# Query and key projections of two blocks as seven block products in place of eight

## The reference

```python
qkv = x @ w_qkv.T                                   # 4096 x 512 by 512 x 1536
q, k, v = ...                                       # 16 heads of 32
q = q * cos + rotate_half(q) * sin                  # the same for k
scores = einsum(q, k) * scale                       # causal, window of 64
x = layernorm(x + softmax(scores) @ v @ w_out.T)
gate, up = silu((x @ w_gate) * s_gate), (x @ w_up) * s_up
x = layernorm(x + ((gate * up) @ w_down) * s_down)
```

## Time and profile before

| | before |
|---|---|
| median of 3 runs | 1202.55 us |
| profiled execution, its own time | 1202.61 us |
| its span (first to last instruction) | 1200.7 us |
| PE busy | 1186.8 us, 99% |
| DVE busy | 844.7 us, 70% |
| ACT busy | 572.7 us, 48% |
| POOL busy | 501.4 us, 42% |
| granted TensorE clock | 0.998 of full speed |

### The profile page before, as it was taken

One profiled execution on the slowest core, in us unless ns is written; L12 is line 12 of the kernel. 1 busy time (PEld: TensorE's weight loads), 2 busy tenths in 40 slices (PEclk: granted clock), 3 DMA queues, 4 the chain that ended last, 5 costly groups with the idle time before them and its releaser, 6 DMA issues.

```text
span 1200.7 us, 24567 instructions
## 1 busy us (share of the span) xinstructions
PE 1186.8 (99%) x8311; PEld 548.7 (46%) x8311; DVE 844.7 (70%) x2546; ACT 572.7 (48%) x1613; POOL 501.4 (42%) x488
## 2 busy tenths in 40 slices
PE   9899999999999999999999999999999999999997
PEld 4344444444444444444444444444444444444444
DVE  7888887548975499655996559865697657975534
ACT  3853883038820388104880149701596016850330
POOL 0745653145522555234561345514465134541330
PEclk9999999999999999999999999999999999999999
DMA  8999764086530855209651195412944139532000
GB/s 283 167 204 233 163 127 84 35 145 120 90 74 36 159 106 107 58 37 165 117 97 49 45 180 103 97 41 66 180 89 89 41 90 173 89 72 53 18 1 36
DMA packets 344409, 123.76 MB, mean 103 GB/s; under 512 B 309472, under 2 KB 328288, under 8 KB 344288
## 3 DMA queue, kind: packets, MB, share of 16 engines
q1 hardware_dynamic: 336128, 107.27, 46.0%
q10 hardware_dynamic: 5040, 8.59, 1.9%
q0 software_dynamic: 3120, 6.29, 1.8%
HBM read 26.69 MB, written 8.39 MB: 29 GB/s over the span
## 4 chain that ended last, share of the span: by engine, by line
PE 92%; DVE 2%; ACT 2%; DMA 1%; issue 1%; POOL 1%; SPq 0%; POOLq 0%; ACTq 0%
PE bank L625 45%; PE bank L770 18%; PE bank L631 16%; PE bank L649 8%; PE bank L732 3%; PE bank L712 2%; ACT bank L940 1%; DMA wqkv<-w_qkvT 1%; DMA xT_sb<-xT_sb 1%; DVE fuse L1052 0%; DVE fuse L1065 0%; POOL xT_sb L513 0%; POOL fuse L518 0%; ACT fuse L895 0%; ACT wu L895 0%
## 5 line engine op out<-in xcount | busy, mean ns | idle before, releaser
L625 PE MATMUL bank<-x1T,wg 128*128 128x512 f16 (+1 forms) x1032 | 242.5, 378 | 0.0
L625 PE MATMUL bank<-x1T,wu 128*128 128x512 f16 x1024 | 241.9, 379 | 0.0
L631 PE MATMUL bank<-wqkv,xT_sb 128*128 128x512 f32 x512 | 229.4, 596 | 0.0
L940 ACT ACTIVATE bank<-bank,neg_max,qk_scale 128x128 f32<-128x128 f32 x512 | 220.5, 435 | 13.0 <-DVE neg_max L1110 11.3
L770 PE MATMUL bank<-wd,fuse 128*128 128x512 f16 (+1 forms) x1056 | 222.4, 373 | 0.0
L518 POOL TENSOR_TENSOR fuse<-ffn_tmp,fuse 128x512 f16<-128x512 f32 x128 | 148.3, 1159 | 156.1 <-ACT fuse L895 155.2
L538 POOL TENSOR_TENSOR fuse<-fuse 128x512 f16<-128x512 f32 x116 | 132.1, 1167 | 129.6 <-ACT fuse L895 128.8
L895 ACT ACTIVATE fuse<-fuse 128x512 f16<-128x512 f32 x120 | 65.6, 618 | 248.2 <-DVE fuse L1060 247.1
L770 PEld LDWEIGHTS bank<-wd,fuse 128*128 128x128 f16 x1056 | 103.4, 98 | 120.3 <-issue 4.0
L513 POOL TENSOR_TENSOR xT_sb<-probs,xT_sb 128x512 f16<-128x512 f32 x112 | 129.7, 1158 | 65.7 <-ACT xT_sb L895 65.7
L625 PEld LDWEIGHTS bank<-x1T,wu 128*128 128x128 f16 x1024 | 100.2, 98 | 120.6
(11 more groups left out here) (147 smaller groups left out, 1097.2 us busy)
## 6 DMA issues: line engine op xcount, KB each, us to landing
xT_sb<-xT SPq DMA_DIRECT2D x32, 256.0 KB, 3.8
v_cross<-v_own SPq DMA_DIRECT2D x64, 128.0 KB, 2.6
out<-y ACTq DMA_DIRECT2D x32, 256.0 KB, 2.0
qkT<-x SPq DMA_DIRECT2D x28, 256.0 KB, 3.4
wqkv<-w_qkvT SPq DMA_DIRECT2D x2, 1024.0 KB, 8.4
wg<-w_gate POOLq DMA_DIRECT2D x1, 2048.0 KB, 9.1
wu<-w_up POOLq DMA_DIRECT2D x1, 2048.0 KB, 11.0
wd<-w_down POOLq DMA_DIRECT2D x1, 2048.0 KB, 9.0
```

The source lines that it names most:

```text
L625: last = pe.matmul(dst, lhsT, rhs, start=(i == 0), stop=(i == len(pairs) - 1))
L631: last = pe.matmul(dst, xT_sb[:, j, k, :], wqkv[:, k, cols], start=(k == 0), stop=(k == KC - 1))
L940: last = act.activation(unit, unit, ACT.Exp, bias=neg_max[:, s % 2, h // 3, h % 3:h % 3 + 1], scale=qk_scale[:, 2:3], accum_out=row_sum[:, ...
```

## The change

Two blocks of a tile make a pair (blocks 0 and 1, blocks 2 and 3). Their x is a 2 by 2 matrix of quarters (front or back block; low or high half of the 512 inputs), as is the q and k weight (low or high inputs; even or odd columns). Strassen's scheme in Winograd's form gives the four results from seven quarter products, with four sums of x, four of the weights and seven of the products.

- PE: `project_pair` replaces the even and odd products of two blocks. The order is products 1, 6, 5, 7, then 2 (after ACT has kept product 1, into the same bank), 3 (after DVE has read banks) and 4. In the body v 1 comes first, then pair 1, then v 2.
- POOL: four sums of x for each pair (`sum_x`, 128x256 each), ahead of `spread_maximum`; four sums of the weights, once (`sum_w`; in tile 0 at steps 9, 10 and 12, and one after `invert_deviation1(a, 2)`); two sums of kept products for each pair (`sum_back`), ahead of the pair's `split_low`.
- ACT: two copies from PSUM for each pair (`keep_products`): for pair 0 ahead of the last y store of the tile, for pair 1 after v 0 and v 1, ahead of the split of block 2.
- DVE: five sums for each pair, of a bank and a kept product. Two (`sum_second`) come before `carry_keys`, the tables and the last `finish_y`. Block 2i+1 reads its odd columns from `kept_products(i)[3]`, in SBUF (`fuse`, or `ffn_tmp`), where it read a bank.
- Tile 1's pair 0 is still made in `first` by the old functions, and tile 0 is unchanged. So 13 pairs change.
- In the diff `sum_x`, `sum_w` (128x1024 each step) and `sum_back` are POOL's, `project_pair` PE's, `keep_products` ACT's and `rope_pair` DVE's.
- The scratch for DMA descriptors made by POOL is set to 4 KB, which makes room for `w_sums`.

```diff
+        w_sums = sb("w_sums", [P, 3, KC // 2, EMB], F32)
+        def kept_products(i):
+            if i == 0:
+                return rope_other[0], rope_other[1], rope_other[3], rope_other[2]
+            return rope_t[0], ffn_tmp[:, 0, :], rope_t[1], ffn_tmp[:, 1, :]
...
+            def sum_x(a, i):
...
+                done(x_summed, pool.tensor_tensor(sums[:, 0, :, :], back_low, back_high, ALU.add))
+                done(x_summed, pool.tensor_tensor(sums[:, 2, :, :], front_low, back_low, ALU.subtract))
+                pool.wait_ge(x_summed[0], n + 1)
+                done(x_summed, pool.tensor_tensor(sums[:, 1, :, :], sums[:, 0, :, :], front_low, ALU.subtract))
+                pool.wait_ge(x_summed[0], n + 3)
+                done(x_summed, pool.tensor_tensor(sums[:, 3, :, :], front_high, sums[:, 1, :, :], ALU.subtract))
+            def sum_w(step):
...
+            def sum_back(a, i):
+                first, second, fourth, seventh = kept_products(i)
+                wait(seventh_kept, pool, a - 1, turn_of(i))
+                wait(pair_summed, pool, a - 1, 5 * turn_of(i) + 1)
+                done(back_summed, pool.tensor_tensor(second, second, seventh, ALU.add))
+                done(back_summed, pool.tensor_tensor(seventh, seventh, fourth, ALU.add))
...
+            def project_pair(a, i):
...
+                wait(*((proj_read, pe, a - 1, NB - 1) if i == 0 else (rope_read, pe, a, 0)))
+                done(first_product, quarter(front_even, front_low, low_even))
+                if i:
+                    wait(rope_read, pe, a, 1)
+                    pe.wait_ge(w_summed, 4)
+                pe.wait_ge(x_summed[0], 8 * (a - 1) + 4 * turn + 4)
+                done(sixth_product, quarter(back_even, sums[:, 1, :, :], w_sums[:, 0, :, :]))
+                done(fifth_product, quarter(front_odd, sums[:, 0, :, :], odd_less_even))
+                done(seventh_product, quarter(back_odd, sums[:, 2, :, :], w_sums[:, 1, :, :]))
+                wait(first_kept, pe, a - 1, turn)
+                done(second_product, quarter(front_even, front_high, high_even))
+                wait(pair_summed, pe, a - 1, 5 * turn + 1)
+                done(qk_done, quarter(front_odd, sums[:, 3, :, :], high_odd))
+                done(qk_done, quarter(back_even, back_high, w_sums[:, 2, :, :]))
...
+            def keep_products(a, i):
...
+                if i:
+                    wait(qk_low, act, a, 0)
+                wait(first_product, act, a - 1, turn)
+                done(first_kept, copy(first, front_even))
+                wait(seventh_product, act, a - 1, turn)
+                done(seventh_kept, copy(seventh, back_odd))
...
+            def rope_pair(a, i):
+                turn = turn_of(i)
+                sum_front_even(a, i)
+                wait(pair_summed, dve, a - 1, 5 * turn + 2)
+                rope_products(a, 2 * i, True, range(2), paired=True)
+                sum_front_odd(a, i)
+                wait(back_summed, dve, a - 1, 2 * turn + 1)
+                if i:
+                    sum_back_even(a, i)
+                wait(pair_summed, dve, a - 1, 5 * turn + 3)
+                rope_products(a, 2 * i, True, range(2, 4), paired=True)
+                rope_sums(a, 2 * i, True)
+                if i == 0:
+                    sum_back_even(a, i)
+                wait(pair_summed, dve, a - 1, 5 * turn + 4)
+                rope_products(a, 2 * i + 1, True, paired=True, odd_rows=kept_products(i)[3])
+                rope_sums(a, 2 * i + 1, True)
...
-    nc = bacc.Bacc("TRN2", target_bir_lowering=False, num_devices=1)
+    nc = bacc.Bacc("TRN2", target_bir_lowering=False, num_devices=1, dynamic_dma_scratch_size=4096)
```

More of the change, by code:

```diff
@@ L583, in body @@
                 if attn:
-                    for j in range(1, NB):
+                    split_low(a, 1, ffn)
+                    sum_back(a, 1)
+                    for j in range(2, NB):
                         split_low(a, j, ffn)
@@ L602, in body @@
                     if more:
+                        for i in range(2):
+                            sum_x(a + 1, i)
                         spread_maximum(a)
@@ L659, in project_odd, with quarter @@
                     done(qk_done, last)
+            def project_pair(a, i):
+                front_even, front_odd, back_even, back_odd = pair_banks(i)
+                front_low, front_high, back_low, back_high = x_quarters(i)
+                low_even, odd_less_even, high_even, high_odd = w_quarters()
+                sums, turn = x_sums(i), turn_of(i)
+                def quarter(dst, lhsT, rhs):
+                    return product(dst, [(lhsT[:, k, :], rhs[:, k, :]) for k in range(KC // 2)])
+                for j in (2 * i, 2 * i + 1):
+                    wait_xT(pe, a, j)
+                wait(*((proj_read, pe, a - 1, NB - 1) if i == 0 else (rope_read, pe, a, 0)))
[12 more added lines that the diff above has]
+                done(qk_done, quarter(back_even, back_high, w_sums[:, 2, :, :]))
             def project_v(a, j, ffn, parts=range(KC)):
@@ L832, in body @@
                 if attn:
[L833 to L836, removed]
+                    project_v(a, 1, ffn)
+                    project_pair(a, 1)
+                    project_v(a, 2, ffn)
                     scores(a, 0, ffn)
@@ L883, in body @@
                 if more:
-                    for j in range(2):
-                        project_even(a + 1, j, ffn)
-                        project_odd(a + 1, j, ffn)
+                    project_pair(a + 1, 0)
                     project_v(a + 1, 0, ffn)
@@ L989, in body @@
                     keep_v(a, 0, ffn)
-                    for j in range(2, NB):
-                        keep_v(a, j - 1, ffn)
-                        split_high(a, j, ffn)
+                    keep_v(a, 1, ffn)
+                    keep_products(a, 1)
+                    split_high(a, 2, ffn)
+                    keep_v(a, 2, ffn)
+                    split_high(a, 3, ffn)
                     exponentials(a, 0, ffn)
@@ L1018, in body @@
                 for j in range(NB):
+                    if more and j == NB - 1:
+                        keep_products(a + 1, 0)
                     wait(y_ready, act, f, j)
@@ L1340, in body @@
                 if attn:
[L1341 to L1346 removed]
+                    split_v(a, 0, ffn)
+                    split_v(a, 1, ffn)
+                    sum_second(a, 1)
+                    rope_pair(a, 1)
                     maxima(a, 0, ffn)
```

101 lines of the change are left out of this document (85 added, 16 removed).

## The result

The changed kernel takes 1273.24 us (median of 4 runs, 1270.54 to 1276.37), the kernel before 1202.38 us beside it: a ratio of 1.059, 95% interval 1.056 to 1.062. Forecast were 1241 us and "slower"; the direction is right, the size is half of what came. The profiled execution is 1276.37 us, 73.8 more than that of before.

A forecast was written before the change was run, and what follows sets the result against it. TensorE, busy for 99% of the span, was taken to bound the kernel. The profiled 1202.6 us plus 6 tiles x 5.0 plus 8.5 for tile 1 gave 1241.1 us, range 1205 to 1253.

The forecast's parts named there:

- What goes: On PE, 13 quarter products of 1.72 us each go: 22.3 us, 1.9%, if nothing waits.
- Step 1: POOL's eight x sums delay the maximum's all-reduce by 2.0 us; PE waits 1.2 us for ACT's copy in pair 0.
- Step 2: DVE and POOL take turns in pair 0's rotation, block 1 takes 7.2 us; PE waits 1.8 us at pair 1's copy.
- Step 3: From pair 1's end, rotations and the chain to unit 1's weights take 20.7 us; a tile is 5.0 us slower.
- the whole 5.0 is lost: Behind scores 4 in each tile: the 5.0 us delay is lost in full and no further delay follows.
- Tile 1: v 1 waits 3.1 us, a POOL weight sum delays DVE by 1.4; scores 4 comes 8.5 us later (3.7 to 10).
- SyncE's queue: Transposes of block 3 go out 6.2 us later; probabilities land near 585.3, PE wants them at 586.2: hidden, only just.
- A: Rival: the waits are covered, so the saved PE work shows; 1183 us, chance 0.13.
- B: Rival: no turns between DVE and POOL, kept products cost what PSUM ones do, SyncE's queue decides; 1208 us, chance 0.17.
- C: Rival: half-width POOL sums cost near 1.16 us (1265), or smaller scratch makes POOL wait for its loads (1261); chance 0.10.
- The prediction's 1.57 us: Time for one DVE operation with two SBUF inputs and one POOL operation, taking turns; four turns in block 1.

The follow-up runs named there:

- e10: e6 with SyncE's four transposes of x1 ahead of those of block 0, from tile 2 on; 1191.4 us, ratio 0.989 to 0.993 against the kernel before.
- e1: The changed kernel with its two longest PE waits filled by repeated work (product 7 of pair 1 twice, step 1's up product three times); 1268.6 us.
- e12: The kernel before with one added PE wait in every tile, for unit 1's weights ahead of the gate product of step 1; 1226.1 us.
- e2: The changed kernel with product 7 left in its bank and DVE making both sums of kept products, in place of ACT's copy and POOL's sums; 1246.5 us.
- e4: The changed kernel with ACT's copies of product 1 earlier in its order, and DVE's sum_second of pair 1 ahead of the splits of v; 1247.8 us.
- e5: The changed kernel with the x sums for tile 1's pair 1 moved on POOL from ahead of block 0's splits to behind invert_deviation1(a, 2); 1272.3 us.
- e11: e7 with the x1 transposes first as in e10, and ACT's split of block 3 behind unit 0's exponentials and the copy of v 3; 1249.3 us.
- e8: e7 with scores 4 moved on PE behind the gate and up products of step 2; 1229.7 us.
- e7: The changed kernel with e2, e4 and e5 together, and pair 1's x sums moved behind the last 1/sqrt of y in every tile; 1235.3 us.
- e6: The changed kernel with seven products for pair 0 alone (product 7 in its bank, product 1 kept early), pair 1 made by eight as before; 1213.2 us.
- e9: The kernel before with the DMA descriptor scratch of 4 KB and nothing else of the change; 1202.4 us, ratio 1.0003.

## Why the prediction was wrong

**What goes.** Right: 1.72 us a quarter product (e10).

**Step 1, sums of x.** Mechanism right, too small. The all-reduce starts 16.0 us after the down projection where it was 13.4, 2.6 late and not 2.0; y's chain is 3.0 late, and PE waits 1.6 to 2.1 us, not 1.2. The term that was mis-sized is the half-width sum: 0.60 was taken, but POOL's rows have 0.73 alone (0.69 from start to start) and 0.81 to 1.17 beside DVE; the eight took 6.8 us for the 6.2 forecast. (The bounds given for this lateness, 0.7 and 5.5 us, come to 0.6 and 5.0 by the prediction's own terms.) Three of the eight:

```profile
532.98 0.91 POOL L587 TENSOR_TENSOR ffn_tmp<-xT_sb 128x256 f32<-128x256 f32 x1
533.85 1.17 POOL L589 TENSOR_TENSOR ffn_tmp<-ffn_tmp,xT_sb 128x256 f32<-128x256 f32 x1
...
537.49 0.73 POOL L589 TENSOR_TENSOR probs<-probs,xT_sb 128x256 f32<-128x256 f32 x1
```

**Step 2, the rotation.** Right in kind: block 1 takes 6.6 us (576.35 to 582.92) for 7.2 forecast, and POOL's four splits 5.93. PE's wait is 2.52 for 1.8.

**Step 3, the chain to scores 4.** From the end of pair 1 (594.82) to the weights of unit 1 are 20.3 us, forecast 20.7. The wait is there, 5.1 us for the 5.6 forecast, but in two parts: 1.41 at scores 2, which the prediction had not seen, and 3.65 at scores 4.

**The step that failed** is the sentence "the whole 5.0 is lost; after it DVE is as far behind PE as before and nothing more comes". More came: TensorE's clock. The prediction priced waits at their length. A tile was forecast at +5.0 and came at +10.0: 3.2 of the difference is the clock at 1.2 GHz behind two of the waits (e1, e12), 0.8 the waits themselves (9.4 against 8.6), and 1.0 the small pitches and rounding. Together with two falls in tile 1 the clock is 23 of the 35 us that the profiled execution lies above the forecast. The page of before could not show it: PE had no wait in tiles 2 to 7 there, two of 0.9 and 0.2 us in tile 1, and its granted clock was 0.998.

**Tile 1** came at +14.0 for +8.5. v 1 waited 7.9 us and not 4.5, and two clock falls, 1.9 and 1.6 us, came on top; against them, the waits behind pair 1 are 0.6 shorter than forecast and tile 0 is 0.9 shorter. For v 1, DVE's read of the last output projection came 4.0 us later than before, since POOL split block 0 3.6 us later, beside DVE's sums. Two things stand ahead of these splits: wu's load, issued 4.4 us later than before (93.2 for 88.8), and the x sums of pair 1 (3.2 us), where the prediction priced only the weight sum. The runs don't put it down to the sums alone. Where wu was issued early, v 1 waited 5.2 us with the sums ahead (e2 at 87.8, e4 at 88.2) and 4.4 and 4.3 with the sums moved (e5 at 89.6, e11 at 87.5). Where it was issued late, v 1 waited 7.3 with the sums ahead (e1 at 92.9), and 8.4 and 9.0 with the sums moved (e8 at 92.9, e7 at 95.1). So the order is worth at most some 0.8 us, and most of the surplus goes with the late issue, whose cause is open.

**SyncE's queue** "hidden, but only just": right, and the most useful line of the prediction; it decided e1, e6 and e11, and e10 turned on it.

**The rivals.** A (covered) and B (no turns) fell with PE's waits and DVE's 1.6 us rows. C fell by e9 and by 6.8 us for eight sums, 0.85 each. The range ended at 1253: the bounds of the unknown costs were added up without one for the clock.

## What to carry over

Price a new wait of a saturated TensorE at its length and, from some 2 us on, at 1.6 to 1.9 us more where the clock falls behind it; work that is done for nothing in the wait can be cheaper than the wait (e1). Work taken off the bounding engine is worth its pitch only where the chain behind it has as much slack: here pair 0 had it and pair 1 did not, and the same scheme on pair 0 alone won 0.9%. Before an order is changed to shorten one chain, follow each queue that stands behind the moved instruction to its last entry (e11), and look for entries whose data are ready long before (e10).

## What the runs showed of the hardware

A pause of 2.66 us on an otherwise full TensorE brought its clock from 2.4 to 1.2 GHz in five of seven cases, the pauses of 3.65 us at scores 4 in all seven, those of 1.41 us at scores 2 in none. In between it goes either way: in e2 the clock fell behind 1.93 us in pair 0 of tile 2 and stayed up behind 2.21 us in tile 3; in e8 it fell behind 1.85 us in tile 5, and in e6 it stayed at 1.00 behind 2.77 us in tile 6. The length of the pause alone doesn't decide it.

A DVE instruction with two SBUF inputs does not always get its turn beside POOL: two of them took 2.37 us beside the splits in the kernel before, and in e7 the first alone stood for 5.83 us (95.63 to 101.46), until the fourth split had ended. The prediction's 1.57 us for one instruction of each holds only where they alternate.

DVE operations with one SBUF input take turns with POOL too, which I had not counted: the tables' and y's tensor_scalar beside POOL's sums in the changed kernel,

```profile
567.75 1.36 DVE L1410 TENSOR_SCALAR tables<-tables,qk_scale 128x256 f32<-128x256 f32 x1
569.15 1.37 DVE L1374 TENSOR_SCALAR y<-y,mean_var,rstd 128x512 f32<-128x512 f32 x1
```

and with POOL idle in e2:

```profile
559.44 0.35 DVE L1405 TENSOR_SCALAR tables<-tables,qk_scale 128x256 f32<-128x256 f32 x1
559.82 0.55 DVE L1369 TENSOR_SCALAR y<-y,mean_var,rstd 128x512 f32<-128x512 f32 x1
```

The Trainium skill's "SBUF — State Buffer" (Who interferes with whom) names tensor_scalar, in its faster modes, among the operations that lock GpSimd out and are locked out by it. By that rule these two take turns if they run in such a mode; which mode they ran in no row shows, but the trace agrees, with 1.0 us lost by one and 0.8 by the other.
